# Attention scores of tiles 0 to 3 in the FFN's PSUM banks, first keys loaded through two queues, and a new order of the steps

## The chip, the cores and the metric

The kernel runs on one core of a Trainium2 chip. The metric is the device time of one execution in microseconds; the figure for a kernel is the median of its runs. A profile is one further execution, recorded by the hardware profiler; it has a span, from the first to the last instruction, and a time of its own.

## What is computed

Sixteen sequences of 64 rows of 256 numbers pass through two layers, all in float32. `x` is (16, 64, 256), `ctx` (16, 64, 64).

```python
x = x + L0_xattn(layernorm(x), ctx, ctx)      # 32 query heads on 8 key heads of 8, no mask
x = x + L0_ffn(layernorm(x))                  # 2 experts of 1024, one chosen per row, squared leaky ReLU
x = x + L1_xattn(layernorm(x), ctx)           # 16 heads of 16, projections Wq, Wkv, Wout, causal mask
x = x + L1_ffn(layernorm(x))                  # see below
```

The last FFN narrows a row to 128, sends it through the two best of 8 experts (hidden 128 to 512, GELU before and between) and a shared one, widens it again and adds a second path through `core_w`. In the reference every expert runs on every row, with a zero input where it isn't chosen, so that its biases add a constant row: `gelu(b1) @ w2 + b2`. The kernel computes those rows once ("rows for zero inputs").

## The kernel before

The 1024 rows lie in SBUF as 8 tiles of 128 rows (two sequences each); two tiles make one of 4 groups for the FFNs. The parts `attn0` and `attn1` run per tile, `ffn0` and `ffn1` per group. Each part is cut into steps with short names. For `attn0` and a tile t: `v` (mean and variance on VectorE, DVE, then the power of -0.5 on GpSimd, POOL), `ln` (normalised queries, DVE), `q` (TensorE, PE, turns the queries; ScalarE, ACT, copies them to QT0), `c` (POOL makes key blocks Z0: the transposed keys KR0 times a 0/1 column `quarter0`, for two halves c = 0, 1 of 128x512), `s` (PE: scores into four PSUM banks), `h` (DVE: largest of each row, four reductions), `m` and `t` (shifts for the softmax, turned by PE, spread by DVE), `k` (POOL: the same blocks from the queries, into the same Z0), `p` (PE: shifted scores, transposed), `f` (ACT: exp), `b` (ACT: values in place), `o` (PE: products with the values), `u` (ACT copies), `n` (PE turns, DVE divides, POOL adds to X). `attn1` is alike, with a `kv` step that makes keys and values on PE. In `ffn0` the rows are normalised (`v`, `ln`), turned (`x`), routed (`r`, `g`), and eight blocks of `u` (up, PE; ACT; square on POOL) and `d` (down, PE) follow. In `ffn1`: `x`, `r`, `e`, `t`, `g` the routing, `d` the narrowing with GELU, `c` and `w` up and down, `y` the sum over experts (DVE), `k` and `o` the widening; `b` and `z` make the rows for zero inputs, once, in 40 small matmul records.

PSUM has eight banks: S (4), H (2), Y (2), each a ring: a step on PE claims the next bank and waits until the step that used it before has been read. `ring_of` names the ring: H and Y belong to the FFNs, S to all else, but scores of attn0's tiles 0 and 1 use H and Y.

The order of the steps on PE, ACT, DVE and POOL is computed when the program is built, by `make_orders`. It walks through an estimated time with `COST` (us of each step by engine), `LOADED` and `LOADED_X` (when loads are taken to have landed) and, among the steps of an engine that could start within `SLACK` of the earliest, takes the one of the greatest worth: the length of what depends on it plus its number in `URGENCY` (one per tile or group); `SWITCH` and `CHANGE` are taken off where ACT would need another table or PE another tiling. Each engine then executes its list strictly in order, waiting on semaphores. SP issues the loads in a fixed order: rows 0, rows 1, C, rows 2 to 3, the later keys, rows 4 to 7, the transposed context CT, WKV, the FFN0 weights and so on; ACT issues the first keys (tiles 0 and 1) as four transfers. `link` makes DVE or POOL wait for the end of its own instruction.

## Time and profile before

| | |
|---|---|
| median of 3 runs | 371.69 us (370.42 to 371.99) |
| profiled execution | 371.51 us, of it span 369.5 us |
| PE (matmuls) | 337.8 us busy, 91% of the span |
| DVE, ACT, POOL | 177.1, 141.7 and 134.3 us busy |

Busy shares are means over the span; what counts is where PE idles. Line 1270 is the helper through which nearly all matmuls are recorded, so the tiles that an instruction writes and reads tell the step.

### The profile page before, as it was taken

The numbers are of one execution on the slowest core, as the hardware profiler recorded it, in microseconds if no ns is written. First come the engines' busy times: TensorE is split into PE (matmuls) and PEld (weight loads), VectorE is DVE, ScalarE is ACT, GpSimd is POOL, SyncE is SP. The second block draws the span as 40 slices with busy tenths as digits, with TensorE's granted clock in tenths as the row PEclk, the third lists the DMA queues.
The fourth block names the chain that finished last, engine by engine and source line by source line (L and its number), as shares of the span: only waits on it lengthen the run. The fifth ranks groups of instructions, "written<-read, shape, count | busy, mean of one in ns | idle before, by whom it ended". The sixth has DMA issues, their size and how long they took to land.

```text
span 369.5 us, 8414 instructions
## 1 busy us (share of the span) xinstructions
PE 337.8 (91%) x3442; PEld 267.2 (72%) x3442; DVE 177.1 (48%) x478; ACT 141.7 (38%) x319; POOL 134.3 (36%) x177
## 2 busy tenths in 40 slices
PE   0667699999999999999999998999999999988995
PEld 0336486778876788787867886689878968976884
DVE  4763762395853036726092419252775441553132
ACT  3136034511413633264213221454557456443540
POOL 5688645472742434554252536130152000100000
PEclk9996899999999999999999999999999999997998
DMA  7996000000000000000000000000000000000000
GB/s 223 305 393 280 2 0 2 4 0 2 2 2 0 2 4 2 2 2 0 2 1 3 2 1 2 2 2 0 2 28 2 2 30 2 2 0 28 2 0 28
DMA packets 6708, 12.61 MB, mean 34 GB/s; under 512 B 2448, under 2 KB 5008, under 8 KB 5904
## 3 DMA queue, kind: packets, MB, share of 16 engines
q1 hardware_dynamic: 6352, 11.83, 9.3%
q8 instruction: 27, 0.44, 0.5%
q10 hardware_dynamic: 320, 0.26, 0.2%
q14 instruction: 9, 0.07, 0.1%
HBM read 11.04 MB, written 1.05 MB: 33 GB/s over the span
## 4 chain that ended last, share of the span: by engine, by line
PE 80%; DVE 11%; POOL 2%; ACT 2%; issue 2%; DMA 1%; ACTq 1%; DVEq 0%; POOLq 0%
PE Y L1270 28%; PE S L1270 24%; PE H L1270 23%; DVE MN L1062 2%; PE S L1346 2%; DVE MN L1083 1%; DMA KR<-in_ctxT 1%; PE S L1355 1%; PE S L1454 1%; POOL X L931 1%; ACT L829 1%; DVE ACC L1233 1%; POOL Z L892 1%; POOL Z L900 1%; ACTq L693 1%
## 5 line engine op out<-in xcount | busy, mean ns | idle before, releaser
L1270 PE MATMUL H<-XT,WF 128*128 128x256 f32 x256 | 61.2, 384 | 0.0
L1270 PE MATMUL Y<-WP,A 128*128 128x256 f32 x256 | 61.2, 384 | 0.0
L1270 PEld LDWEIGHTS H<-XT,WF 128*128 128x128 f32 x256 | 47.0, 190 | 9.2 <-issue 2.7
L1270 PEld LDWEIGHTS Y<-WP,A 128*128 128x128 f32 x256 | 46.7, 190 | 8.5 <-issue 2.7
L814 ACT ACTIVATE R<-H 128x512 f32<-128x512 f32 x32 | 19.1, 598 | 76.4 <-PE H L1270 75.2
L842 ACT ACTIVATE A<-H,B 128x256 f32<-128x256 f32 x84 | 35.7, 472 | 31.7 <-PE H L1270 26.3
L947 POOL TENSOR_TENSOR A<-R 128x512 f32<-128x512 f32 x32 | 33.6, 1051 | 36.4 <-ACT R L814 19.5
L1270 PEld LDWEIGHTS Y<-W,A 128*128 128x128 f32 x336 | 43.4, 191 | 4.6 <-issue 2.4
L1270 PE MATMUL Y<-W,A 128*128 128x128 f32 x336 | 45.1, 277 | 0.8 <-DVE ACC L1233 0.5
L1270 PE MATMUL H<-GH,W 128*128 128x256 f32 x168 | 42.9, 381 | 0.5 <-ACT GH L831 0.5
L1233 DVE SCALAR_TENSOR_TENSOR ACC<-Y,gate,ACC 128x128 f32<-128x128 f32 x64 | 22.4, 350 | 41.9 <-PE Y L1270 40.5
L1270 PEld LDWEIGHTS H<-GH,W 128*128 128x128 f32 x168 | 29.2, 191 | 3.2 <-issue 0.7
L906 POOL TENSOR_TENSOR Z<-KT,quarter_ 128x512 f32<-128x512 f32 x16 | 16.4, 1049 | 31.5 <-ACT KT L799 31.5
L906 POOL TENSOR_TENSOR Z<-QT,quarter_ 128x512 f32<-128x512 f32 x16 | 16.4, 1053 | 22.6 <-PE S L1270 22.6
L784 ACT ACTIVATE PT<-S 128x512 f32<-128x512 f32 x32 | 16.5, 602 | 16.2 <-PE S L1270 16.2
L879 POOL TENSOR_TENSOR rstdf<-varef,mhalf 128x2 f32<-128x2 f32 x8 | 5.6, 701 | 42.9 <-DVE varef L1024 42.9
L892 POOL TENSOR_TENSOR Z<-KR,quarter 128x512 f32<-128x512 f32 x16 | 16.3, 1040 | 8.8 <-PE S L1270 6.5
L900 POOL TENSOR_TENSOR Z<-QT,quarter 128x512 f32<-128x512 f32 x16 | 16.3, 1040 | 7.8 <-PE Y L1270 4.4
L879 POOL TENSOR_TENSOR rstd<-vare,mhalf 128x1 f32<-128x1 f32 x16 | 8.7, 550 | 25.4 <-DVE vare L1024 25.4
L1270 PEld LDWEIGHTS S<-PT,V 64*32 64x32 f32 x1024 | 14.1, 112 | 5.3 <-ACT PT L784 2.6
L1270 PE MATMUL S<-PT,V 64*32 64x128 f32 (+1 forms) x1024 | 16.9, 267 | 1.1 <-ACT PT L784 1.1
L1083 DVE TENSOR_REDUCE MN<-S 128x8 f32<-128x512 f32 x16 | 10.2, 685 | 15.7 <-PE S L1270 15.6
(173 smaller groups left out, 498.2 us busy)
## 6 DMA issues: line engine op xcount, KB each, us to landing
W<-in_w SPq DMA_DIRECT2D x2, 1344.0 KB, 10.3
WF<-in_wf SPq DMA_DIRECT2D x2, 1024.0 KB, 11.6
WP<-in_wp SPq DMA_DIRECT2D x2, 1024.0 KB, 13.9
out_dram<-X SPq DMA_DIRECT2D x8, 128.0 KB, 1.7
KR<-in_ctxT SPq DMA_DIRECT2D x4, 192.0 KB, 3.8
X<-in_x SPq DMA_DIRECT2D x1, 512.0 KB, 7.8
X<-in_x SPq DMA_DIRECT2D x2, 128.0 KB, 2.3
KR<-in_ctxT ACTq DMA_DIRECT2D x4, 64.0 KB, 3.2
```

The costliest lines, as they stand in the source:

```text
L784: nc.scalar.activation(flat(PT[:, t % 2, 8 * c:8 * c + 8, :]), b[:, :], ACT.Exp, scale=HD0 ** -0.5).then_inc(done, 1)
L814: nc.scalar.activation(R0[:, n % 2, :], b[:, :], ACT.Prelu, alpha=0.5).then_inc(done, 1)
L842: ins = nc.scalar.activation(A1[:, n % 4, :], b[:, k * GT:(k + 1) * GT], ACT.Gelu, bias=B1[:, ch:ch + 1])
L879: nc.gpsimd.tensor_tensor(dst, src, mhalf[:, 0:dst.shape[1]], ALU.pow).then_inc(rstd_ready, 1)
L892: nc.gpsimd.tensor_tensor(Z0[:, t % 2, c, :, :], KR0[:, c, t * P:(t + 1) * P].unsqueeze(1).to_broadcast([P, 4, P]), quarter0[:, :].unsquee ...
L900: nc.gpsimd.tensor_tensor(Z0[:, t % 2, c, :, :], QT0[:, t % 2, c, :].unsqueeze(1).to_broadcast([P, 4, P]), quarter0[:, :].unsqueeze(2).to_ ...
L906: nc.gpsimd.tensor_tensor(Z1[:, t % 2, :, c, :], src[:, t % 2, c, :].unsqueeze(1).to_broadcast([P, 4, P]), quarter_[:, :].unsqueeze(2).to_ ...
L947: nc.gpsimd.tensor_tensor(flat(A0[:, n % 2, :, :]), R0[:, n % 2, :], R0[:, n % 2, :], ALU.mult).then_inc(a0_ready, 1)
L1062: nc.vector.tensor_reduce(MN[:, slot("attn0", t), 8 * c:8 * c + 8], b[:, :].rearrange("p (h t) -> p h t", t=S), AX.X, ALU.max, negate=True ...
L1083: nc.vector.tensor_reduce(MN[:, slot("attn1", t), 8 * c:8 * c + 8], b[:, :].rearrange("p (h t) -> p h t", t=S), AX.X, ALU.max, negate=True ...
L1233: ins = nc.vector.scalar_tensor_tensor(ACC[:, k, :], b[:, k * L:(k + 1) * L], gate[:, k, e:e + 1], ACC[:, k, :], ALU.mult, ALU.add)
L1270: return nc.tensor.matmul(o, a, b, start=start, stop=stop, skip_group_check=shared)
```

## The change

Scores of attn0's tiles 2 and 3 go to the H and Y banks as well. The first keys are issued half by SP, between rows 0 and rows 1, and half by ACT. A new step `a` of attn0, for tiles 0 and 1, makes the second half of the key blocks (c = 1) on ACT as four scaled copies of 128x128; POOL makes the first half only. In `expert` (ffn1's `y`) the wait of DVE for its own first accumulation is dropped but for the last expert. Costs, load times, slack and the whole urgency table are new, and with them the order on all four engines; among these `z` has a low urgency now. The urgency table of attn1 is left out here.

```diff
--- before.py
+++ after.py
@@ -62,7 +62,7 @@
 
 def ring_of(s):
 
-    if (s[0], s[2]) == ("attn0", "h") and s[1] < 2:
+    if (s[0], s[2]) == ("attn0", "h") and s[1] < 4:
         return "HY"[s[3] // 2]
     return FILLS.get((s[0], s[2]))
 
@@ -72,59 +72,59 @@
 
 
 COST = {
-    "const": dict(e="dve 1.6 act .6", i="pool 1.7", m="pool 3.9", g="pool 2.5"),
-    "attn0": dict(c="pool 2.1", v="dve .83 pool .56", ln="dve .52", q="pe .22 act .37", s="pe 1.06", h="dve .69",
-                  k="pool 2.1", m="dve .6", t="pe .06 dve 1.2", p="pe 1.4", f="act .6", b="act .45", o="pe 1.05", u="act .37",
-                  n="pe .45 dve .82 pool .8"),
+    "const": dict(e="dve 1.7 act .9", i="pool 1.4", m="pool 5.0", g="pool 1.6"),
+    "attn0": dict(a="act 1.1", c="pool 2.08", v="dve .83 pool .56", ln="dve .52", q="pe .22 act .37", s="pe 1.06", h="dve .69",
+                  k="pool 2.08", m="dve .6", t="pe .06 dve 1.2", p="pe 1.6", f="act .6", b="act .45", o="pe 1.05", u="act .38",
+                  n="pe .45 dve .82 pool .88"),
     "attn1": dict(kv="pe .97 act .76", c="pool 2.1", v="dve .83 pool .55", ln="dve .41",
                   x="pe .22 act .37", w="pe .89 act .37", s="pe 1.58", h="dve .69", k="pool 2.1",
-                  m="dve .38", t="pe .06 dve 1.2", p="pe 1.4", f="act .6", o="pe .67", u="act .37", n="pe .45 dve .71",
+                  m="dve .45", t="pe .06 dve 1.2", p="pe 1.58", f="act .6", o="pe .67", u="act .37", n="pe .45 dve .71",
                   a="pe .22 act .37", r="pe .87 dve .42"),
     "ffn0": dict(v="dve 1.52 pool .7", ln="dve .74", x="pe .45 act .59", r="pe .9 dve .55", g="act .2 dve 1.05",
                  u="pe 1.73 act .6 pool 1.05", d="pe 1.73", y="dve 1.0"),
     "ffn1": dict(v="dve 1.53 pool .7", ln="dve .77", x="pe .45 act .59", i="pool 1.43", r="pe .9 dve .59",
-                 e="act .2 dve 2.56", t="act .2 dve 1.1", d="pe .87 act 1.13", g="pe .25 act .3", c="pe .86 act .94",
-                 w="pe .43", y="dve .56", k="pe .25 act .37", o="pe 1.3 dve .42", b="act .22 pool .4", z="dve .3 pe 2.4 act .25")}
+                 e="act .2 dve 3.0", t="act .2 dve 1.1", d="pe .87 act 1.13", g="pe .25 act .3", c="pe .86 act .94",
+                 w="pe .43", y="dve .60", k="pe .25 act .37", o="pe 1.3 dve .42", b="act .22 pool .4", z="dve .3 pe 2.4 act .25")}
 COST = {part: {s: [(e, float(d)) for e, d in zip(text.split()[::2], text.split()[1::2])] for s, text in costs.items()}
         for part, costs in COST.items()}
 GATE = 0.44
-LOADED = {("attn0", "c"): 4.4, ("attn0", "b"): 6.5, ("ffn0", "x"): 11.0, ("ffn0", "u"): 20.0, ("attn1", "kv"): 12.0,
-          ("ffn1", "z"): 34.0, ("ffn1", "r"): 27.0, ("ffn1", "b"): 27.0, ("ffn1", "c"): 37.0, ("attn1", "w"): 24.0}
-LOADED_X = [2.8, 3.6, 7.0, 7.0, 9.5, 9.5, 9.5, 9.5]
+LOADED = {("attn0", "a"): 5.2, ("attn0", "c"): 5.2, ("attn0", "b"): 6.0, ("ffn0", "x"): 13.0, ("ffn0", "u"): 24.0, ("attn1", "kv"): 14.0,
+          ("ffn1", "z"): 60.0, ("ffn1", "r"): 28.0, ("ffn1", "b"): 29.0, ("ffn1", "c"): 37.0, ("attn1", "w"): 26.0}
+LOADED_X = [2.6, 4.9, 7.0, 7.0, 11.5, 11.5, 11.5, 11.5]
 LATENCY = {"pe": 0.24, "act": 0.08, "dve": 0.07, "pool": 0.08}
 TABLE_LOAD = 1.3
 TILED = {("attn0", "s"), ("attn0", "p"), ("attn0", "o"), ("attn1", "kv"), ("attn1", "s"), ("attn1", "o")}
 MODE_CHANGE = 0.09
-SWITCH = 489.77
-CHANGE = 324.38
-SLACK = {"act": 0.020, "dve": 0.532, "pe": 0.030, "pool": 0.361}
+SWITCH = 6525.99
+CHANGE = 355.33
+SLACK = {"act": 0.331, "dve": 0.564, "pe": 0.034, "pool": 3.752}
 GELU = {("ffn1", s) for s in "bdc"}
 EXP = {("attn0", "f"), ("attn1", "f"), ("ffn0", "g"), ("ffn1", "e"), ("ffn1", "t")}
 URGENCY = {
-    "const": "e 770; i -628; m -305; g 218",
-    "attn0": "k 151 703 839 755 708 910 288 179; t 564 -334 -83 134 169 -662 629 -31; "
-             "c 999 999 244 999 999 321 999 531; v 643 244 387 -483 -540 -739 -997 -485; "
-             "ln -609 -592 -929 143 -919 -66 149 164; q 304 889 -782 -582 135 -800 -844 -999; "
-             "s -344 65 -560 777 -297 687 880 999; b -429 -524 -654 -872 -900 -563 15 999; "
-             "p -449 576 359 297 -634 855 414 509; o 179 769 -219 733 688 -105 163 414; "
-             "n -416 281 -918 119 -252 -246 -271 198; h -43 147 264 209 489 486 -433 449; "
-             "m 416 999 999 999 999 999 999 998; f 999 948 987 -524 -420 -71 -588 -999; "
-             "u 44 -719 -703 546 407 607 555 451",
...
-    "ffn0": "v 998 380 999 994; ln 560 236 621 493; x 85 -734 -157 674; r 773 387 -873 -822; "
-             "g -776 204 -849 -76; u -998 -999 -999 -999; d -999 -962 -999 -486; y -783 -953 -988 -988",
-    "ffn1": "v -457 595 -279 -873; ln -550 -628 -623 -267; x 555 313 346 180; i 990 696 353 572; "
-             "r -840 -613 599 146; e 654 999 994 634; t 462 -882 143 -54; d 553 999 906 467; g 94 -906 -922 -803; "
-             "c -549 200 755 -344; w 136 614 670 206; y 999 -444 -795 -986; o 405 982 679 940; b -285; z 702; "
-             "k 367 357 186 647"}
+    "const": "e 803; i 812; m -565; g 579",
+    "attn0": "a 250 -818; k 895 894 138 272 -665 -582 -947 -939; t 999 464 669 947 906 151 249 -206; "
+             "c 551 -999 -187 -195 -801 -593 164 -363; v 687 218 -263 -161 935 -694 -147 -18; "
+             "ln -999 909 87 794 273 999 817 999; q -757 -999 -823 -423 -277 -544 190 -561; "
+             "s -975 -731 -266 -521 917 881 632 645; b -814 -855 -448 -804 797 797 999 679; "
+             "p -541 983 78 756 767 698 590 614; o 568 663 665 838 506 561 533 415; "
+             "n 888 939 999 -452 822 -528 -511 -486; h 672 -155 -999 -827 -219 907 398 158; "
+             "m 999 202 -604 -972 -841 -562 -999 -999; f 999 999 999 943 999 522 999 862; "
+             "u 606 896 -160 883 376 739 896 896",
...
+    "ffn0": "v -357 -772 365 -408; ln 999 970 999 834; x 335 580 525 474; r 726 891 171 -169; "
+             "g -146 40 -370 -838; u -807 -891 -911 -823; d 352 128 303 140; y 492 195 176 -235",
+    "ffn1": "v -959 -438 -718 390; ln -953 653 -96 -318; x -807 -765 -980 413; i 875 872 869 719; "
+             "r 511 120 975 249; e 564 206 276 -77; t 28 482 359 913; d -411 290 -17 496; g 267 328 503 832; "
+             "c 382 -579 -64 -633; w 940 773 786 487; y -341 -386 585 561; o 999 999 999 999; b 172; z -862; "
+             "k 311 384 290 -345"}
 URGENCY = {part: {words[0]: [float(w) for w in words[1:]] for words in map(str.split, text.split(";"))}
            for part, text in URGENCY.items()}
 BODIES = [("ffn0", g) for g in range(GROUPS)] + [("ffn1", g) for g in range(GROUPS)]
@@ -133,6 +133,8 @@
 def work_of(s):
 
     parts = list(COST[s[0]][s[2]])
+    if (s[0], s[2]) == ("attn0", "c") and s[1] < 2:
+        parts = [(e, d / 2) for e, d in parts]
     if s[0] == "ffn1" and s[2] == "w":
         e, c = WORK[s[3]]
         if c == CH1[e] - 1 and e == EXPERTS[-1]:
@@ -185,6 +187,9 @@
         add(a("ln"), a("v"))
         add(a("q"), a("ln"))
         add(a("s"), a("c"), a("q"))
+        if t < 2:
+            add(a("a"))
+            need(a("s"), a("a"))
         add(a("k"), a("s"))
         add(a("m"), a("h", 3))
         add(a("t"), a("m"))
@@ -201,6 +206,7 @@
             need(a("p"), ("const", 0, "e", 0))
             need(a("t"), ("const", 0, "e", 0), part=1)
             need(a("c"), ("const", 0, "e", 0), of=0)
+            need(a("a"), ("const", 0, "e", 0), of=0)
             need(a("b"), ("const", 0, "i", 0))
         if t >= 2:
             for later, first in (("c", "p"), ("v", "ln"), ("ln", "q"), ("q", "p"), ("f", "o"), ("b", "o"), ("o", "n")):
@@ -626,6 +632,7 @@
         x0_ready = sem("x0_ready")
         q_ready = sem("q_ready")
         kz_ready = sem("kz_ready")
+        kz_half = sem("kz_half")
         qz_ready = sem("qz_ready")
         kz1_ready = sem("kz1_ready")
         qz1_ready = sem("qz1_ready")
@@ -686,10 +693,10 @@
         SMALL = 9
         KEYS = [(0, 2), (2, TILES)]
 
-        def keys(eng, k):
+        def keys(eng, k, places=range(4)):
             first, last = KEYS[k]
             rows_of = ctxT.rearrange("(c q) n -> q c n", c=DC)
-            for r in range(4):
+            for r in places:
                 eng.dma_start(KR0[r:P:4, :, first * P:last * P], rows_of[:, :, first * P:last * P]).then_inc(ld_k[k], 16)
 
 
@@ -700,6 +707,7 @@
                              ).then_inc(ld_x[first], 16)
 
             rows(0, 1)
+            keys(sp, 0, (0, 1))
             rows(1, 2)
             sp.dma_start(C[:, :, :], ctx_in.rearrange("(t p) d -> p t d", p=P)).then_inc(ld_c, 16)
             rows(2, 4)
@@ -769,6 +777,15 @@
                     nc.scalar.copy(V2[:, t % 2, :, part, 16 * part:16 * part + HD0],
                                    C[:, t, :].rearrange("p (k d) -> p k d", d=HD0)).then_inc(v2_ready, 1)
 
+            def key_blocks0(t, _):
+
+                if t == 0:
+                    act.wait_ge(places_ready, 1)
+                    act.wait_ge(ld_k[0], 16 * 4)
+                for i in range(4):
+                    nc.scalar.activation(Z0[:, t % 2, 1, i, :], KR0[:, 1, t * P:(t + 1) * P], ACT.Copy, scale=quarter0[:, i:i + 1]
+                                         ).then_inc(kz_half, 1)
+
             def places0(*_):
 
                 act.wait_ge(places_ready, 1)
@@ -851,8 +868,8 @@
                     filled(act, "ffn1", g - 1, "k", 0)
                 nc.scalar.activation(flat(ACC[:, :, :]), b[:, 0:GT], ACT.Copy, scale=0.1).then_inc(done, 1)
 
-            keys(act, 0)
-            run("act", h | {("attn0", "f"): probs0, ("attn0", "b"): values0, ("const", "e"): places0, ("attn1", "f"): probs1, ("attn1", "kv"): keys1,
+            keys(act, 0, (2, 3))
+            run("act", h | {("attn0", "f"): probs0, ("attn0", "b"): values0, ("attn0", "a"): key_blocks0, ("const", "e"): places0, ("attn1", "f"): probs1, ("attn1", "kv"): keys1,
                      ("ffn0", "g"): exps("ffn0", E0), ("ffn0", "u"): leaky, ("ffn1", "e"): exps("ffn1", E1),
                      ("ffn1", "t"): top_exp, ("ffn1", "b"): gelu_biases, ("ffn1", "d"): inner, ("ffn1", "x"): turned_rows1,
                      ("ffn1", "c"): hidden, ("ffn1", "y"): shared})
@@ -888,7 +905,7 @@
                 if t >= 2:
 
                     filled(pool, "attn0", t - 2, "f", 3)
-                for c in range(DC):
+                for c in range(DC if t >= 2 else 1):
                     nc.gpsimd.tensor_tensor(Z0[:, t % 2, c, :, :], KR0[:, c, t * P:(t + 1) * P].unsqueeze(1).to_broadcast([P, 4, P]),
                                             quarter0[:, :].unsqueeze(2).to_broadcast([P, 4, P]), ALU.mult).then_inc(kz_ready, 1)
 
@@ -1232,7 +1249,7 @@
                 for k in range(2):
                     ins = nc.vector.scalar_tensor_tensor(ACC[:, k, :], b[:, k * L:(k + 1) * L], gate[:, k, e:e + 1], ACC[:, k, :],
                                                          ALU.mult, ALU.add)
-                    if k == 0 or j == E1:
+                    if j == E1:
                         link(ins)
                 if j == E1:
                     ins = nc.vector.tensor_tensor(flat(ACC[:, :, :]), b[:, GT:2 * GT], flat(ACC[:, :, :]), ALU.add)
@@ -1280,7 +1297,9 @@
 
                 claims_ = [claim(pe, "attn0", t, "h", i) for i in range(4)]
                 read_out(pe, "attn0", t, "q", 0)
-                pe.wait_ge(kz_ready, 2 * t + 2)
+                pe.wait_ge(kz_ready, t + 1 if t < 2 else 2 * t)
+                if t < 2:
+                    pe.wait_ge(kz_half, 4 * t + 4)
                 for c in range(DC):
                     for i, (b, done) in enumerate(claims_):
                         quarter = slice(32 * i, 32 * i + 32)
```

## Rows read from the trace of the kernel before

**Rows 1.** The page: busy time by engine; busy tenths in 40 slices of 9.24 us.
```profile
PE 337.8 (91%) x3442; PEld 267.2 (72%) x3442; DVE 177.1 (48%) x478; ACT 141.7 (38%) x319; POOL 134.3 (36%) x177
...
PE   0667699999999999999999998999999999988995
...
DMA  7996000000000000000000000000000000000000
```

**Rows 2.** Busy time by stage: stretch, its length, engines, PE's granted clock, DMA share.
```profile
0.00:48.74 48.74, 28.06 (x390) 18.04 (x391) 27.02 (x72) 14.64 (x37) 33.08 (x62) 0.89 0.67 228
48.74:328.09 279.35, 275.79 (x2870) 220.08 (x2868) 136.20 (x359) 113.20 (x253) 101.25 (x115) 1.00 0.01 3
328.09:342.55 14.46, 11.70 (x49) 9.13 (x49) 7.04 (x29) 5.16 (x11) 0.00 (x0) 0.76 0.05 18
...
358.65:369.50 10.85, 6.16 (x26) 4.74 (x25) 3.37 (x9) 0.43 (x2) 0.00 (x0) 0.84 0.07 24
...
26.19:34.30 8.11, 6.96 (x175) 5.30 (x176) 1.25 (x5) 3.65 (x10) 7.55 (x9) 0.58 0.98 383
```

**Rows 3.** The chain of waits up to the first FFN: start, us, what.
```profile
2.83 4.00 DMA KR<-in_ctxT
...
6.96 2.05 POOL Z L892 x2
...
9.14 0.70 PE H L1270 x4
...
11.15 2.50 DVE MN L1062 x4
...
14.91 0.69 PE S L1276 x2
...
15.60 2.07 PE S L1270 x6
17.67 0.63 PE H L1270 x4
...
22.14 0.91 DVE MS L1072
...
23.07 0.99 DVE MS L1073
...
26.19 1.99 PE S L1270 x36
...
37.42 2.04 POOL Z L900 x2
...
40.71 0.90 PE S L1454 x4
...
48.74 3.51 PE H L1270 x16
```

**Rows 4.** Timeline of the first 16 us: issues (ACTq), copies, rstd, a wait.
```profile
0.74 2.70 ACTq L693 DMA_DIRECT2D KR<-in_ctxT  x4
...
5.08 0.29 ACT L776 CAST ofbank<-bank 64x128 bf16<-64x128 f32 x1
...
6.10 0.37 ACT L735 COPY QT<-S 128x256 f32<-128x256 f32 x1 [0.41 <-PE S L1276]
...
10.95 1.08 POOL L879 TENSOR_TENSOR rstd<-vare,mhalf 128x1 f32<-128x1 f32 x2
...
15.60 0.92 PEld L1270 LDWEIGHTS S<-CT,WKV 64*128 64x128 f32 x4 [0.40 <-DMA WKV<-in_wkv]
```

**Rows 5.** Timeline: scores of tile 2, and the rows for zero inputs.
```profile
36.08 1.12 PE L1270 MATMUL S<-Z,QT 32*64 32x256 f32 x32 [1.22 <-DVE O L1110]
...
41.54 5.92 PE L1270 MATMUL S<-W,GB 128*9 128x128 f32 x40
```

**Rows 6.** The last group: eight down matmuls in the chain; four accumulations on the timeline.
```profile
344.57 0.89 PE Y L1270 x8
...
358.75 1.51 DVE L1233 SCALAR_TENSOR_TENSOR ACC<-Y,gate,ACC 128x128 f32<-128x128 f32 x4 [0.59 <-PE Y L1270]
```

18 rows, old and new, of the table URGENCY are left out of this document.

## The prediction

> **What bounds the kernel now.** I read the page's busy shares and slices first, then busy time by stage, then the chain of work that ended last, then the timeline of the first microseconds. TensorE (PE) is busy 337.8 us, 91%, but that is an average over unlike stages [rows 1]. By stage [rows 2], PE idles 48.74 - 28.06 = 20.7 us before the first FFN matmul, 279.35 - 275.79 = 3.6 us in the long middle, 14.46 - 11.70 = 2.8 us at the last group's entry and 10.85 - 6.16 = 4.7 us at the end. The middle is PE-bound: there another order of the same work can hardly win, only lose. The change can win in the prologue, which is a chain of dependences.
>
> That chain [rows 3]: the first keys land at 6.83; POOL makes both halves of tile 0's key blocks by 9.01; scores(0) start at 9.14; DVE reduces them from 11.15 to 13.65; tile 1's queries are turned on PE at 14.91; keys and values of attention 1 follow from 15.60; scores(1) only at 17.67; probabilities(1) at 26.19; the first FFN's rows are turned at 40.71; the zero-input rows start at 41.54 and take 5.92 [rows 5]; the first FFN block starts at 48.74 [rows 3].
>
> **First keys, two queues.** ACT issues four transfers in 2.70 us, the last at 2.83, landing 4.00 later [rows 3, 4]. Two issues on ACT end about 2.1; SP issues rows 0 (to about 1.2), then its two, the last starting near 1.9. So the last issue is 2.83 - 1.9 = about 0.9 us earlier. With the same 4.00 us flight the gain is 0.9; with less traffic in front (C, 256 KB, and rows 2 to 3 are now issued behind the keys) the flight could be shorter. I take 1.2, bounds 0.9 and 1.8. The transfer engines are busy 0.7 of the first slice, the one in which the keys fly, and 0.9 or more in the next two [rows 1]. The Trainium skill, DMA: Bandwidth & Descriptors, section Issuing engines are not separate DMA queues, says that queues of several engines share the same 16 transfer engines and save only issue time. By that rule this term is the bare 0.9 and the time below 0.3 us longer; no row before shows a split transfer.
> The price: everything behind on SP is issued about 2 x 0.675 = 1.35 us later (2.70 for four, [rows 4]) (rows 1, C, rows 2 to 7, the other keys, the weights). Rows 1 are needed only after tile 0's statistics. The weights for attention 1's first keys are what PE waits for at 15.60 now [rows 4]; they come up to 1.35 later, but that step no longer has to precede scores(1), see below. All loads end within slice 3, before 37 us [rows 1], the FFN0 weights ahead of the larger W1 and W2. I cost this at nothing; where the step stays in front, 1.35.
>
> **Half of the first key blocks on ScalarE.** POOL's two multiplies take 2.05 [rows 3]; now one, 1.03, while ACT does four 128x128 copies scaled per partition. No such row exists: a 64x128 copy takes 0.29, a 128x256 copy 0.37 [rows 4]. Four cost 1.2 to 1.5; I take 1.2, nearest the 128-column row. The copy of the turned queries (0.37) may stand behind them on ACT, whereas now it is done at 6.47, before the keys land. Landing 5.6 + 0.1 + 1.2 + 0.4 + 0.1 puts scores(0) at about 7.4 instead of 9.14: 1.7 us won with the keys' term (bounds 1.0 and 2.5). Without the ACT half a plain early landing would give 1.2.
>
> **Order anew: scores(0) to scores(1).** Now 17.67 - 9.14 = 8.5 us: scores 1.99, reductions 2.50, shifts, tile 1's normalised rows, their turn 0.69, then keys and values 2.07 [rows 3]. Tile 1's rows are late because POOL, multiplying key blocks of 1.03 from 6.96 on [rows 3], comes to its rstd at 10.95 [rows 4]. In the new table tile 1's key blocks fall from 999 to -999 and `v` of tile 1 hardly moves (244 to 218), so its rstd goes in front of them; `ln` of tile 1 rises from -592 to 909. Then scores(1) need only the four FFN banks back, which are free when reductions(0) end: 1.99 + 2.50 + 0.1 = 4.6. Query blocks(0) (895) may precede key block(1) on POOL, and that half, 1.03, could come up to 0.5 late. I take 5.1 in place of 8.5: 3.4 won, bounds 0 (the order keeps keys and values in front) and 3.9.
>
> **Scores(1) to the first FFN.** Scores(1) to probabilities(1) take 26.19 - 17.67 = 8.5 now and hold the same steps after; I count 0.5 for shifts(1), which take 1.9 (0.91 and 0.99) [rows 3] against the 1.26 between the end of reductions(0), 13.65, and the turn at 14.91, tile 1's rows included, bounds 0 and 1.0. From 26.19 to 40.71 are 14.5 us: value products at a granted clock of 0.58, results, POOL additions, rstd behind 2.04 us of query blocks [rows 2, 3]. A new order may put POOL's masks or another multiply in front of the addition; or not. I take 0, bounds -2 and +2.
>
> **Zero rows late; tiles 2 and 3 in the FFN banks.** The zero rows take 5.92 us [rows 5], 0.148 for each of 40. At the rate of 128-column matmuls later (0.89 for eight, [rows 6]) 40 cost 4.45; the difference is a stretch at the lower of PE's two levels, 1.2 GHz in place of 2.4, after the idle time in front of 40.71. So moving them removes no work that PE need not do; it can save 0 to 1.5. What takes their place pays the same half clock when PE idled before it, so I take 0. Scores of tile 3 can now run inside the prologue's idle time without holding the S banks: 1.12 us of PE work [rows 5] out of the saturated stretch; I take 0.5, bounds 0 and 1.1.
>
> **The dropped DVE wait.** Of each pair of accumulations the first one no longer waits for its own end, but for the last expert: 28 waits fewer. Four in a row take 1.51, 0.38 each [rows 6]; they lie on the path once, at the end, elsewhere under PE. Nothing to 0.38; I take 0.
>
> **Sum.** 1.7 + 3.4 + 0.5 + 0 + 0 + 0.5 = 6.1 us less before the FFN. The middle has 3.6 idle us now; a new order with the same work can make that 2 to 7; I give back 0.6. The profiled execution took 371.51 (span 369.5 and 2.0 around it), the median 371.69, so both serve: 371.5 - 5.5 = 366.0. All low bounds (1.0, 0, 0, -2, 0, 0, and 3.4 given back) make 375.9; all high ones (2.5 + 3.9 + 1.0 + 2 + 1.5 + 1.1, a tail unchanged) make 359.5.
>
> **Rivals.**
> *The FFN waits for DVE.* Scores of tiles 2 and 3 now fill H and Y, which the first FFN block must claim. If they are queued on PE before it, it waits until DVE has reduced both, 2 x 2.5 us [rows 3], where before scores(2) lay in S and only PE's order mattered. For: DVE is busy 27.0 us of the prologue [rows 2], and a shorter one needs about the same. Against: with tile 3's reductions 29.6 fit into some 37 us (48.74 less 6.1 and the zero rows' 5.9), and the table puts tiles 2 and 3 last (-999, -827) among reductions. If it decides, up to 5.0 of the 5.5 go: 369 to 371.5.
> *The gain is used up at the end: slower.* The last group's entry, with no attention work left to fill it, costs 2.8 idle us and runs at a mean granted clock of 0.76 [rows 2]: 0.48 of 14.46, 6.9 us, at the 1.2 GHz level, of which some 5.5 busy lose half, 2.7; about 5.5 in all. The two entries before it lie in the middle, whose 3.6 idle us show that attention 1 of later tiles fills them. A new order that spends this filler earlier, in the place of the zero rows, bares both entries: 11 - 5.5 = 5.5 slower, 377. It decides once more than the prologue's gain is lost: two bare entries, not one (that gives 371.5). For: PE's total is fixed, what goes early is missing late. Against: the last tiles' attention 1 can't start before the last FFN0 group ends.
> *More than counted.* Probabilities(0) no longer wait behind keys and values, so the half-clock stretches of the prologue vanish too, and 1.5 of the zero rows is won: 361 to 363.
>
> **How the numbers follow.** Forecast 0.58 (363 to 369, likeliest 366.0); more than counted 0.10; FFN waits for DVE, or one bare entry, 0.20 (369 to 372); slower through two bare entries 0.12 (374 to 378). Half a per cent, 1.9 us, is about what can be told from no change: faster means below 369.8, slower above 373.6. A third of the third case lies below 369.8: faster 0.75, same 0.13, slower 0.12. The range 361.5 to 372.5 leaves out the slower case and a little of the fastest.
>
> **What would show it.** Right: key blocks on POOL and ACT start at 5.3 to 5.9; scores(0) at 7.0 to 7.6; scores(1) at 12 to 13, in front of the keys and values; probabilities(1) near 20; FFN rows turned near 35; first FFN block within 3 us of that; PE idle before it about 14 in place of 20.7; middle below 5. Wrong: keys landing later than 6.3, an ACT copy above 0.5, PE waiting for keys-and-values weights in front of scores(1), a wait of the first FFN block on DVE's reductions, or a second entry with PE below full clock after 200 us.

## The result and the profile after

The changed kernel takes 361.97 us, the median of 4 runs (360.95 to 363.05), beside 371.40 for the kernel before on the same chip (4 runs, 370.42 to 371.99): a ratio of 0.976, 95% interval 0.9727 to 0.9793. Forecast were 366.0 with a range of 361.5 to 372.5, and faster as the likeliest case. The range held, only 0.5 us from its lower end. Of two profiles the first took 363.05 (span 361.2); its rows follow. The one of before took 371.51 (span 369.5), so 8.3 us of span are to be explained. In all that follows, executions over 1.5% longer than the fastest of the same kernel on the same chip are left out of medians and ratios.

The page of the kernel after, its first line and the slices of PE and of the granted clock (9.03 us each), answers to [rows 1]:

```profile
PE 334.9 (93%) x3442; PEld 266.5 (74%) x3442; DVE 176.1 (49%) x478; ACT 148.8 (41%) x331; POOL 132.1 (37%) x175
...
PE   2577699999999999999999999999999999997994
...
PEclk9969779999999999999999999999999999999999
```

PE is busy 2.9 us less and idle 361.2 - 334.9 = 26.3 us in place of 31.7. Where, busy time by stage shows, columns as in [rows 2]: up to the first FFN block, the middle, the last group's entry, its experts, the end; and two stretches of the prologue.

```profile
0.00:46.21 46.21, 28.05 (x487) 17.23 (x487) 36.18 (x76) 20.48 (x53) 34.61 (x64) 0.86 0.69 241
46.21:326.97 280.76, 279.82 (x2792) 225.71 (x2792) 128.56 (x361) 115.60 (x249) 97.47 (x112) 0.99 0.01 3
326.97:335.86 8.89, 6.21 (x29) 4.69 (x29) 5.10 (x22) 3.99 (x10) 0.00 (x0) 1.00 0.09 31
335.86:352.06 16.20, 16.20 (x113) 15.33 (x114) 3.05 (x11) 8.31 (x20) 0.00 (x0) 1.00 0.00 0
352.06:361.20 9.14, 4.66 (x25) 3.55 (x24) 3.19 (x9) 0.37 (x1) 0.00 (x0) 1.00 0.09 30
20.00:26.60 6.60, 6.39 (x79) 4.77 (x79) 4.58 (x10) 1.64 (x5) 5.25 (x5) 0.50 1.03 382
39.50:50.60 11.10, 9.46 (x90) 7.55 (x91) 6.62 (x12) 2.77 (x9) 7.14 (x9) 0.54 0.01 1
```

The entry begins here where the constant rows of group 2 have been added. By that boundary the kernel before has, in the same view:

```profile
48.74:330.88 282.14, 278.44 (x2890) 222.46 (x2888) 138.12 (x366) 114.40 (x254) 101.25 (x115) 1.00 0.01 3
330.88:342.55 11.67, 9.04 (x29) 6.75 (x29) 5.11 (x22) 3.97 (x9) 0.00 (x0) 0.71 0.07 22
```

Stage by stage the difference is -2.5 (prologue), -1.4 (middle), -2.8 (entry), +0.1 (experts) and -1.7 (end; 10.85 before, [rows 2]). The idle time tells more: prologue 20.7 to 18.2, middle 3.7 to 0.9, entry 2.6 to 2.7, end 4.7 to 4.5. The entry and the end have kept their waits; their matmuls ran at the full clock, 1.00 where before shows 0.71 and 0.84. So 5.4 us are idle time of PE that is gone, and 4.2 are PE's rate in the last stages; the middle has 1.4 us more of busy time, and PE's granted clock from 39.5 to 50.6, where its first FFN blocks lie, is 0.54. (In all there are 3442 matmuls as before, but some have changed stage.)

The chain up to the first FFN, of after (start, us, what), answers to [rows 3]:

```profile
4.75 1.38 DVE Q L1059
...
13.63 0.70 PE H L1287 x4
...
20.48 3.71 PE S L1287 x12
...
24.80 1.89 PE S L1287 x64
...
27.79 1.66 PE S L1287 x38
...
46.21 3.62 PE H L1287 x8
```

Scores(1) stand in front of the keys and values now, at 13.63 in place of 17.67. But behind the turned shifts(1) come the keys and values of attention 1 (the x12), tile 2's queries, value products(0) (x64) and scores(2), and only then, at 27.79, probabilities(1), later than the 26.19 of [rows 3].

The timeline of after, issues and first steps, then the rows that come later:

```profile
0.74 1.36 ACTq L700 DMA_DIRECT2D KR<-in_ctxT  x2
1.18 1.40 SPq L700 DMA_DIRECT2D KR<-in_ctxT  x2
4.78 1.28 ACT L786 ACTIVATE Z<-KR,quarter 128x128 f32<-128x128 f32 x4 [0.43 <-DMA KR<-in_ctxT]
4.83 1.04 POOL L909 TENSOR_TENSOR Z<-KR,quarter 128x512 f32<-128x512 f32 x1
...
7.39 0.70 PE L1287 MATMUL H<-Z,QT 32*64 32x256 f32 x4 [0.46 <-ACT QT L743]
...
21.82 1.21 DVE L1094 TENSOR_TENSOR MD<-S,place 128x1024 bf16<-128x1024 bf16 x1
...
40.84 0.66 PE L1473 MATMUL S<-identf,XN 128*128 128x128 f32 x2 [2.14 <-DVE XN L1047]
...
86.19 4.54 PE L1287 MATMUL S<-W,GB 128*9 128x128 f32 x40
```

The waits of PE in the middle, first of the kernel before (48.74 to 330.88), then of the kernel after (46.21 to 326.97): engine and line that waited, for what, us in total, times, longest.

```profile
PE S L1410 <- DVE MS L1093: 1.3, 3, 0.9
PE S L1355 <- ACT OT L735: 0.9, 1, 0.9
PE S L1504 <- DVE gate L1217: 0.8, 1, 0.8
PE S L1270 <- DVE MN L1062: 0.4, 1, 0.4
```

```profile
PE S L1429 <- DVE MS L1110: 0.5, 1, 0.5
PE S L1287 <- DVE MD L1116: 0.4, 1, 0.4
```

These are waits for shifts and results of the attentions and for a gate of the routing: in the new order other matmuls stand in front, and all but 0.9 us of such waits are gone.

### The profile page after: what moved, and what is told of

The parts are those of the page before. It is cut to its first block, busy times and chain, and to the rows that moved or that the text cites. A ratio compares the mean times of both kernels' runs of the same rounds, so it can differ in the third digit from the quotient of the medians.

```text
span 361.2 us, 8428 instructions
## 1 busy us (share of the span) xinstructions
PE 334.9 (93%) x3442; PEld 266.5 (74%) x3442; DVE 176.1 (49%) x478; ACT 148.8 (41%) x331; POOL 132.1 (37%) x175
## 4 chain that ended last, share of the span: by engine, by line
PE 86%; DVE 9%; POOL 2%; issue 1%; ACT 1%; POOLq 0%; DVEq 0%; ACTq 0%
PE Y L1287 30%; PE H L1287 25%; PE S L1287 25%; PE S L1365 2%; DVE MN L1079 2%; PE S L1473 1%; DVE MN L1100 1%; PE S L1374 1%; DVE MS L1090 1%; DVE ACC L1250 1%; POOL Z L909 1%; DVE XN L1047 1%; POOL X L948 0%; PE S L1530 0%; DVE Q L1059 0%
## 5 line engine op out<-in xcount | busy, mean ns | idle before, releaser
L1287 PE MATMUL H<-XT,WF 128*128 128x256 f32 x256 | 62.0, 391 | 0.0
L1287 PEld LDWEIGHTS H<-XT,WF 128*128 128x128 f32 x256 | 48.6, 195 | 8.5 <-issue 1.5
L859 ACT ACTIVATE A<-H,B 128x256 f32<-128x256 f32 x84 | 35.2, 471 | 26.6 <-PE H L1287 26.3
L1250 DVE SCALAR_TENSOR_TENSOR ACC<-Y,gate,ACC 128x128 f32<-128x128 f32 x64 | 19.8, 346 | 38.3 <-PE Y L1287 37.8
L909 POOL TENSOR_TENSOR Z<-KR,quarter 128x512 f32<-128x512 f32 x14 | 14.5, 1050 | 5.5 <-PE S L1287 5.4
L1191 DVE SCALAR_TENSOR_TENSOR X<-Y,G,X 128x256 f32<-128x256 f32 x8 | 3.9, 482 | 25.8 <-PE Y L1287 25.7
## 6 DMA issues: line engine op xcount, KB each, us to landing
W<-in_w SPq DMA_DIRECT2D x2, 1344.0 KB, 10.8
```

Source lines behind the costliest of these rows:

```text
L859: ins = nc.scalar.activation(A1[:, n % 4, :], b[:, k * GT:(k + 1) * GT], ACT.Gelu, bias=B1[:, ch:ch + 1])
L909: nc.gpsimd.tensor_tensor(Z0[:, t % 2, c, :, :], KR0[:, c, t * P:(t + 1) * P].unsqueeze(1).to_broadcast([P, 4, P]), quarter0[:, :].unsquee ...
L1250: ins = nc.vector.scalar_tensor_tensor(ACC[:, k, :], b[:, k * L:(k + 1) * L], gate[:, k, e:e + 1], ACC[:, k, :], ALU.mult, ALU.add)
L1287: return nc.tensor.matmul(o, a, b, start=start, stop=stop, skip_group_check=shared)
```

## The experiments

Each kernel was compared with runs of the kernel before on the same chip. A ratio is to that kernel.

**1. The parts without the order.** The kernel before with keys through two queues, ACT's half and the dropped DVE wait; the order is the old one with the two `a` steps put in.

```diff
+        for t, behind in ((0, ("const", 0, "e", 0)), (1, ("attn0", 0, "q", 0))):
+            orders["act"].insert(orders["act"].index(behind) + 1, ("attn0", t, "a", 0))
...
```

> Everything of the change but the order, the tables and the banks of tiles 2 and 3: keys by two queues, half of the first key blocks on ACT, the dropped DVE wait, in the order of before. If the parts themselves carry the gain (theory of the prediction: 1.7 us from the keys and the ACT half), scores(0) start near 7.4 and the time is 369.5 to 370.5. If the order carries it (rival), tile 1's scores stay behind the keys and values of attention 1, whose weights land no earlier, and the time is 371 to 372.

Measured: 369.80, ratio 1.0005 (0.9962 to 1.0048). The time lies in the range that was expected if the parts carry the gain, but before took 370.10 on this chip: no gain. Timeline:

```profile
8.24 0.70 PE L1283 MATMUL H<-Z,QT 32*64 32x256 f32 x4 [0.46 <-ACT QT L739]
...
15.43 1.22 PE L1283 MATMUL S<-CT,WKV 64*128 64x128 f32 x4 [0.66 <-DMA WKV<-in_wkv]
...
17.43 0.70 PE L1283 MATMUL H<-Z,QT 32*64 32x256 f32 x4
```

Scores(0) came 0.9 earlier than before; then tile 1's rows and the keys and values stood in front of scores(1) as ever, and those start at 17.43, within 0.3 us of where they did (17.67 in [rows 3]).

**2. One part undone at a time.** From the kernel after: all four key transfers on ACT; POOL makes both halves; the zero rows right behind the first FFN rows.

```diff
-            keys(sp, 0, (0, 1))
...
-            keys(act, 0, (2, 3))
+            keys(act, 0)
```

> The changed kernel with all four key transfers issued by ACT again, same order. If the path from the keys to the first FFN sets the time, the keys land 2 us later (6.8 in place of 4.8), scores(0) start near 9.3 and the time is 363.5 to 364. If PE's fill and clock set it, most of the 2 us is absorbed before probabilities(1), and the time is within 0.7 of the changed kernel's, 362 to 362.7.

```diff
...
-                for c in range(DC if t >= 2 else 1):
+                for c in range(DC):
...
```

> The changed kernel with both halves of the key blocks of tiles 0 and 1 on POOL, ACT's step left out, same order. Path theory: scores(0) wait for POOL until about 7.0 instead of the query copy at 7.33, no loss there; tile 1's block comes 1.04 later (14.2), scores(1) at 14.4 in place of 13.63: 0.5 to 1 us slower, 362.5 to 363. Fill theory: no change, 362. If POOL's longer stretch holds up DVE's normalised queries, as the 1.38 us of the changed trace suggest, another 0.5.

```diff
+        Z = ("ffn1", 0, "z", 0)
+        move("pe", Z, ("ffn0", 0, "x", 0))
+        move("act", Z, ("ffn0", 0, "x", 0))
+        move("dve", Z, ("ffn0", 0, "ln", 0))
```

> The changed kernel with the rows for zero inputs moved on PE, ACT and DVE to where before had them, behind the turned rows of the first FFN. If moving them late was worth nothing but the clock (prediction), the time is 362 to 363.5: 4.5 to 6.3 us of PE work merely stands elsewhere. If they held up the FFN's start and its followers (rival), the first block starts at 50 to 52 and the time is 365 to 367.

Measured: 363.38 (ratio 0.9833, 0.9764 to 0.9903), 363.38 (0.9815, 0.9763 to 0.9866) and 363.39 (0.9812, 0.9752 to 0.9873). Each is 1.1 to 1.4 us above the medians of after (361.97, and 362.31 in experiment 6); all intervals overlap: 0.3 to 0.4% by the medians, 0.2 to 0.7% by the ratios, and by the intervals not to be told from nothing. The first lies between its two expectations and the second at the upper end of its own, so neither decides; the third lies in the one that follows the prediction. Of the early zero rows the timeline shows why:

```profile
41.71 7.04 PE L1294 MATMUL S<-W,GB 128*9 128x128 f32 x40
...
50.91 1.97 PE L1294 MATMUL H<-XT,WF 128*128 128x256 f32 x8
```

They take 7.04 us here in place of 4.54 at 86.19, but the first eight FFN matmuls behind them take 1.97. In the kernel after those FFN matmuls are the first and take the half clock: 3.62 in the chain. Whatever comes first pays.

**3. The old order with five steps moved.** Experiment 1 with tile 1's turn behind scores(0) and keys and values behind probabilities(0) on PE, and what feeds them moved alike.

```diff
...
+        move("pe", ("attn0", 1, "q", 0), ("attn0", 0, "s", 0))
+        move("pe", ("attn1", 0, "kv", 0), ("attn0", 0, "p", 0))
+        move("act", ("attn1", 0, "kv", 0), ("attn0", 0, "f", 3))
+        move("dve", ("attn0", 1, "ln", 0), ("attn0", 0, "ln", 0))
+        move("pool", ("attn0", 1, "v", 0), ("attn0", 0, "c", 0))
```

> The run with the old order and the new parts, and in it only five steps moved: tile 1's normalised queries, its rstd and its turn forward, and attention 1's keys and values of tile 0 behind tile 0's probabilities. If the prediction's chain (scores(1) no longer behind the keys and values) carries the gain, scores(1) start at 13.5 to 14 in place of 17.4, probabilities(0) near 15.6, the FFN 3 to 4 us earlier: 366 to 367. If the gain comes from attention work of tiles 2 and 3 that the new order puts into PE's idle time in the prologue (rival), the 3.8 us are lost again before the FFN's rows are turned: 368.5 to 370.

Measured: 364.35, ratio 0.9855 (0.98 to 0.991). Timeline, then two stages:

```profile
12.72 0.70 PE L1291 MATMUL H<-Z,QT 32*64 32x256 f32 x4
...
21.55 0.63 PE L1291 MATMUL S<-MD,ofbank 64*64 64x512 bf16 x8 [1.29 <-DVE MD L1098]
...
35.70 1.09 PE L1477 MATMUL S<-identf,XN 128*128 128x128 f32 x4 [3.52 <-DVE XN L1051]
```

```profile
0.00:44.17 44.17, 26.20 (x389) 16.21 (x390) 27.00 (x71) 16.71 (x45) 31.09 (x60) 0.88 0.73 252
44.17:326.20 282.03, 278.57 (x2891) 222.60 (x2890) 136.32 (x366) 114.67 (x254) 101.38 (x115) 1.00 0.01 3
```

This is the chain of the prediction: scores(1) at 12.72, probabilities(1) at 21.55, FFN rows turned at 35.70. With the parts, which alone gave nothing, five moves carry most of the gain by the medians: some 6 us of 9, more than either expectation had. Idle before the FFN: 44.17 - 26.20 = 18.0, as in after (18.2). What is missing to it is the middle: 3.5 idle us, with the waits of the old order, where after has 0.9.

**4. Scores of tiles 2 and 3 back in the S banks,** all else, the order too, as after (`IN_FFN` is 4 while the orders are made, then 2).

```diff
-    if (s[0], s[2]) == ("attn0", "h") and s[1] < 4:
+    if (s[0], s[2]) == ("attn0", "h") and s[1] < IN_FFN:
```

> The changed kernel, same order, with the scores of tiles 2 and 3 in the S banks as before. If the two extra pairs of banks are what lets attention work fill the prologue, scores(2) wait for the S banks to be read and probabilities(1) for DVE's reductions(2), 2.5 us each for tiles 2 and 3: 365 to 368. If the order alone does it, 362 to 363.

Measured: 372.38, ratio 1.0043 (1.0009 to 1.0076): the whole gain is gone. Timeline:

```profile
31.80 1.07 PE L1293 MATMUL S<-MD,ofbank 64*64 64x512 bf16 x8 [2.84 <-DVE MN L1085]
...
50.40 1.07 PE L1293 MATMUL S<-MD,ofbank 64*64 64x512 bf16 x8 [6.22 <-DVE MN L1085]
...
57.63 1.97 PE L1293 MATMUL H<-XT,WF 128*128 128x256 f32 x8
```

That is worse than either expectation. Probabilities(1) and (2) wait for the S banks that scores(2) and (3) hold until DVE has reduced them. Ahead of the first FFN block PE is busy 33.05 of 57.63 us: against the kernel after 6.4 us more idle and 5.0 more busy, for it also runs at half rate there (the eight at 31.80 take 1.07, in the kernel after 0.63 at 27.79). The banks alone are no gain, but this order can't run without them.

**5. The clock at the end.** The kernel before with unread 128x128 matmuls in PE's gaps of the end: 18 before the sums of groups 2 and 3 are turned, 12 before the last gates. They add work that no result uses.

```diff
+            def warm(b, n):
+                for _ in range(n):
+                    mm(b[:, 256:256 + P], identb[:, :], identb[:, :])
...
+                if g >= 2:
+                    warm(b, 18)
```

> The kernel before with such matmuls only at the end: 18 before the sums of groups 2 and 3 are turned, 12 before the last group's gates are turned. If the half clock in the last 40 us, which the profile before shows and no profile of the changed order does, is chance from run to run, then the runs of before that had it come down to those that had not: 366.5 to 368 throughout, against 370 before. If the half clock there follows from the old order whatever PE does in the gaps, 370 to 371.

Measured: 367.97 beside 370.13 for before, ratio 0.9972 (0.9936 to 1.0008). The widening of group 2 (four matmuls each) takes in this kernel, in before and in after, one line of the timeline each:

```profile
332.23 1.03 PE L1270 MATMUL Y<-CW,GX 128*128 128x256 f32 x4
```

```profile
332.68 1.92 PE L1270 MATMUL Y<-CW,GX 128*128 128x256 f32 x4
```

```profile
328.56 1.03 PE L1287 MATMUL Y<-CW,GX 128*128 128x256 f32 x4
```

The clock can be held there, and that is worth 2.2 us by the medians, from nothing to 2.4 by the interval: less than the 4.2 of the one pair of profiles. The profiles differ too: of the old order, before has 1.9 at both widenings of the end (332.68 and 362.85), experiments 1 and 3 only at the first. Executions of before spread from 366.77 to 371.62 in that comparison, with the added matmuls from 367.00 to 369.37. That would fit a fall that doesn't come in each, which is not shown: of each of these kernels only one execution has a trace.

**6. The half clock of the prologue.** The kernel after again, unchanged; the kernel after with unread matmuls in the gaps of prologue and end, first many narrow ones in the prologue alone, then a quarter as many of 512 columns; and experiment 3 with the zero rows late and the same wide ones. The narrow ones number 30 before queries(0) are turned, 50 and 38 before shifts(0) and (1), 30 before the first FFN rows; the wide ones 8, 13, 10 and 8 at these places, and at the end 5 before the sums of groups 2 and 3 and 3 before the last gates.

```diff
...
+                if t == 0:
+                    warm(b, 30)
...
```

> The changed kernel with matmuls of 128x128 bf16 whose results nobody reads, placed in PE's idle time before tile 0's first turn (30), before the shifts of tiles 0 and 1 (50 and 38) and before the first FFN's rows (30). If the half clock at 20 to 26.6 and 40 to 50.6 follows from PE's idle time in front of it, the granted clock stays at the upper level, 16 us of busy time at half clock shrink by about 7 and scores(0) and (1) by 0.8 each: 355 to 357. If it doesn't follow from it, or the added matmuls delay the steps behind them, 361 to 363.

From the narrow to the wide ones:

```diff
-                    mm(b[:, 256:256 + P], identb[:, :], identb[:, :])
+                    mm(b[:, 0:4 * P], identb[:, :], identb[:, :].unsqueeze(1).to_broadcast([P, 4, P]))
...
-                    warm(b, 30)
+                    warm(b, 8)
...
```

> The kernel after with unread 128x512 bf16 matmuls on PE in its gaps: 8 before the first queries are turned, 13 and 10 before the first two shifts are turned, 8 before the first FFN rows, 5 before the sums of groups 2 and 3, 3 before the last gates. Theory (the half clock of the prologue is left over after the new order and costs 3 to 5 us; the narrower unread matmuls lost 2.6 us of it to a wait that showed as issue): no such wait with a quarter of the instructions, granted clock above 0.9 up to the first FFN, 355 to 358. Rival (the wait has another cause): it stays, 358 to 360.

> The kernel after once more, unchanged, beside the next two on one chip. Theory (some 2.7 us of the gain are the end, where the old order falls to half clock in part of its executions and the new one does not): median 361 to 363, ratio 0.972 to 0.980, and a profile whose widening of group 2 takes 1.03 us for 8 matmuls at a granted clock of 1.00 in the last 35 us. Rival (the new order's end falls too, the first profile was a lucky one): a widening of group 2 near 1.92 and a span of 364 or more.

```diff
...
+        move("pe", Z, ("ffn0", 0, "d", 6))
+        move("act", Z, ("ffn0", 0, "u", 7))
+        move("dve", Z, ("attn0", 3, "n", 0))
...
```

> The old order with five moved steps, the zero-input rows late, and the same unread matmuls. Theory (the short chain, 35.7 to the first FFN rows, and full clock add up): rows turned near 33 to 35, first FFN within 2 us of that, the end warm; 356 to 359. Rival (without attention work of later tiles in the prologue the shorter chain only moves PE's idle time to a later place): first FFN near 36 but a middle with 4 to 7 idle us, 361 to 364.

Measured: narrow 357.91 (ratio 0.9665, 0.9606 to 0.9724), between its two expectations; then on one chip after again 362.31 (0.979, 0.9742 to 0.9837), wide 357.14 (0.9643, 0.9599 to 0.9687), moved steps with wide ones 363.35 (0.982, 0.9768 to 0.9871). The second profile of after ends as the first, its widenings at 1.03. The two stages up to the last entry, of the wide kernel and of the moved steps with wide ones:

```profile
0.00:42.66 42.66, 33.47 (x525) 17.56 (x526) 33.91 (x76) 20.32 (x53) 33.43 (x63) 0.92 0.76 261
42.66:321.31 278.65, 277.75 (x2795) 224.25 (x2795) 129.77 (x362) 115.54 (x249) 98.81 (x113) 1.00 0.01 3
```

```profile
0.00:39.04 39.04, 28.04 (x386) 14.69 (x387) 25.57 (x67) 16.78 (x44) 30.55 (x59) 0.96 0.84 285
39.04:325.95 286.91, 283.45 (x2934) 226.35 (x2934) 137.72 (x372) 114.29 (x255) 101.75 (x116) 1.00 0.01 3
```

With the clock better held, the same order is 5.2 us shorter by the medians, 4.2 by the spans (359.7 of the second profile of after, 355.5): 2.5 ahead of the first FFN block, 1.6 in the stage behind it (45.12 and 280.28 us in the second profile of after), whose first blocks no longer run at half rate. PE has no less time without real work than in that profile (20.0 + 0.9 us against 17.4 + 0.9), so the gain is its rate: the half rate that these matmuls removed cost the kernel after 4 to 5 us. This version beats both kernels. The last one starts its first FFN 3.6 us earlier and takes 6.2 us longer in all; its expected 356 to 359 was wrong, and the rival came true: 361 to 364, since the shorter chain only moves PE's idle time. With the order of experiment 3 the same matmuls bring about 1 us (364.35 to 363.35, on two chips, not clear of noise). Of the wide kernel's 33.47 us some 10.8 are unread matmuls (3.60, 2.97, 2.33 and 1.90), so 22.7 us of real work lie ahead of its FFN; of the other's 28.04 some 12.1 are unread, and 15.9 are real. The start of the first FFN says nothing by itself. Between these two, both mostly at the full rate, what counts is PE's time without real work: 20.0 + 0.9 against 23.1 + 3.5.

## Why the prediction was near, and which of its steps failed

**Keys and ACT's half: the sum right (1.75 for 1.7), both terms off.** The keys' blocks start at 4.78, not 5.6: from the start of the last issue, near 1.9 as forecast, the transfer took 2.9, not 4.00. The term was 2.05, above its bound of 1.8. The Trainium skill (DMA: Bandwidth & Descriptors, Issuing engines are not separate DMA queues) says that issuing from several engines saves the issue time alone. That would be the bare 0.9 of the prediction, less than half of what was measured. But rows 1, C and rows 2 to 3 are now issued behind the keys, and with all four on ACT, where the keys land at 6.69 again, in front of or beside the last of them: whether the second queue or the traffic shortened the flight was not separated, so the rule is neither borne out nor refuted here. ACT's copies took 1.28 for 1.2. But the normalised queries took 1.38 on DVE in place of 0.51, and scores(0), at 7.39 as forecast, waited for their turn on PE and copy on ACT, not for the blocks; with both halves on POOL they start at 7.24. That the two errors cancel in the sum is luck.

**Scores(0) to scores(1): right in kind, 2.3 for 3.4.** Keys and values are no longer in front. The interval is 6.24, not 5.1, 0.9 of the difference because a shift of 0.23 us on the timeline of before takes 1.10 beside POOL's multiply. Experiment 3 has 5.38.

**Scores(1) to probabilities(1): the step that failed.** The prediction said that they "hold the same steps after". They take 14.2 us, not 8.0. DVE had the shifts spread at 21.82 + 1.21 = 23.03; PE then still had keys and values, queries(2), value products(0) and scores(2) in its list, 4.8 us, much of it at a granted clock of 0.50. In the wide kernel of experiment 6, which runs the same list at the full rate, with ten unread matmuls more in a wait, the same stretch takes 10.9 us (12.59 to 23.45), so about half of the 6.2 us too many are the list and half PE's rate. So the rows of the first FFN are turned at 40.84, not near 35 (40.71 in [rows 3]). From probabilities(1) on 13.05 us pass for the 14.5 that were kept, inside its bounds; but the first FFN block stands 5.4 us behind the turn (46.21), not within 3. The chain that I worked out exists, as experiment 3 shows; the new table doesn't make it. It makes PE's waits full instead: scores of tiles 2 and 3, value products and keys and values run before the FFN.

**Zero rows: right.** Moved work is not removed; they take 4.54 late, and their early place costs nothing that can be told (experiment 2).

**Scores of tiles 2 and 3 in the FFN banks: mis-sized.** I gave them 0.5. Taken away under the new order they cost 10 us, half rate included; without that order the question doesn't arise. A term for one edit alone was the wrong form: the banks and the order hold only together.

**The middle: wrong sign.** "Can hardly win, only lose", and 0.6 given back. The order won 2.8 of the 3.7 idle us, the waits listed above: experiment 4, the new order without the banks, keeps 0.9 idle us there, experiment 3, the old order, 3.5. These waits were in the trace of before, each on one line, and could have been read.

**The end: not seen.** I left it as it was. Its idle time did stay, but the profiled pair differs by 4.4 us there, nearly all by the clock; experiment 5 puts the average at 0 to 2.4. Why this order keeps the clock over waits as long as before (1.38 and 1.45 us in both) stays open: all seven profiles of the new order without added matmuls at the end (both of after, experiments 2 and 4 and the narrow one of 6) show full clock in the first widening; before and experiments 1 and 3, with the old, 1.9.

**The rivals.** The FFN waits for no reductions: both scores were done and read by 42.4, and PE has no idle time in front of the first block. A part of that rival holds one step earlier: PE waits 2.14 us at 40.84 for the rows that DVE normalises behind a reduction of tile 3 and beside POOL (last section). No second bare entry came. The time fell among those of the case "more than counted", but not by its mechanism: the half-clock stretches did not vanish, and experiment 6 prices them. The prologue's shortfall (2.5 us of stage, not 6.1) was made good by the middle and the end, neither of which was forecast to gain: that the range held is luck.

**The dropped DVE wait: as said.** Four accumulations on the path take 1.25, not 1.51 (0.26 less), within the bounds of 0 and 0.38.

## What to carry to other kernels

Where one engine holds nine tenths of the span, add up its idle time and its matmuls at half rate over all stages; a milestone that comes earlier (the first FFN block) gains nothing if it leaves work of the same engine behind. An order written anew is read step by step on the in-order queue: ask what stands between two steps of a chain after the change, not only whether their own costs are the same. And where an engine must wait, work without a reader that keeps its clock up can be worth more than a shorter wait: here 4 to 5 us in the new order; in the old one with five moves about 1, not clear of noise.

## What was not expected of the hardware

**DVE beside POOL.** Two pairs of rows of the kernel after, each a DVE instruction under a POOL one, and the normalised rows of the first FFN:

```profile
12.14 1.04 POOL L909 TENSOR_TENSOR Z<-KR,quarter 128x512 f32<-128x512 f32 x1
12.15 1.10 DVE L1090 TENSOR_TENSOR MS<-MN,MS 128x64 bf16<-128x64 f32 x1
...
24.41 2.12 POOL L980 TENSOR_SCALAR_AFFINE_SELECT MD<-MD 64x2048 bf16<-64x2048 bf16 x1
24.91 1.87 DVE L1059 TENSOR_SCALAR Q<-X,mv,rstd 128x256 f32<-128x256 f32 x1 [1.88 <-PE S L1293]
...
39.87 1.87 DVE L1047 TENSOR_SCALAR XN<-X,mvf,rstdf 128x256 f32<-128x256 f32 x2
```

The normalised rows take 0.51 us where POOL is quiet (at 7.43); here 1.87, ending at 26.78, a quarter of a us behind POOL's end at 26.53, and the shift ends 0.07 behind POOL's. The Trainium skill says so (SBUF — State Buffer, SBUF: two separate sides): for a DVE operation in a two-port mode or with two SBUF inputs, the two engines share a pair of ports, which is held for a whole instruction while the other waits. The trace agrees. The earlier key block on POOL (from 4.83) so lengthened a DVE step on the chain by 0.9 us at the start. Later the new order costs more by it: the first FFN's rows take 1.87 at 39.87, where POOL multiplies keys from 39.51 to 43.64, and 0.74 in the kernel before, where POOL's multiply of keys begins only at 40.59:

```profile
40.15 0.74 DVE L1030 TENSOR_SCALAR XN<-X,mvf,rstdf 128x256 f32<-128x256 f32 x2 [0.48 <-POOL rstdf L879]
```

**A clock row that starts late.** Scores(0) take 0.65 to 0.70 us per group of four while the granted clock over them reads 1.00, and 0.39 to 0.45 in the kernel with 3.60 us of unread matmuls ahead, also at 1.00. In every profile of this case the row reads 1.00 from the start until PE's first fall after it had run at the full rate, whatever the durations say. In the kernel after that is until 19.9 us; in experiment 4, where PE runs at half rate until 54 us, the row reads 1.00 throughout. That profiled execution has a mean clock of 1.000 at 372.41 us, and the nine others of the same kernel 0.954 to 0.963 at 370.56 to 373.14. So neither the row nor a run's mean clock tells the rate before that first fall; the durations do.

**A wait that comes with more instructions.** The kernel with narrow unread matmuls has, in the prologue:

```profile
27.43 0.41 PE L1287 MATMUL S<-MD,ofbank 64*64 64x512 bf16 x3 [2.57 <-issue]
```

PE idles 2.57 us though nothing that the trace shows holds it. The profiled execution took 360.77 us, 2.9 more than the median, and no other of this kernel has a trace: whether they have the wait is not shown. With 39 wide ones in their place PE idles 1.34 so at one point (29.57), with the moved steps 1.10 (31.82), in the kernel after nowhere so long. Its cause was not tried.
